# A block of cross-attention and a routed FFN on one core: FFN sums by ScalarE and accumulating DMAs, and another layout of a one-hot table

## The reference

```python
x = x + xattn(layernorm(x), ctx)          # 16 heads of 16, bias on q, k, v, o
xf = layernorm(x)                         # 4096 tokens of 256
shared = silu(xf @ sh_gate.T) * (xf @ sh_up.T) @ sh_down.T      # hidden 512
w, idx = top_k(softmax(xf @ gate_w.T), 2); w = w / sum(w)       # 8 experts
routed = sum over the two picks: w * (silu(xf @ eg[e].T) * (xf @ eu[e].T) @ ed[e].T)
out = x + shared + routed
```

## Time and profile before

| | us |
|---|---|
| median of 3 runs | 719.77 (718.18 to 723.15) |
| the profiled execution's own time | 715.89 |
| its span | 713.9 |
| PE busy | 614.5 (86%) |
| DVE busy | 440.9 (62%) |
| POOL busy | 394.1 (55%) |
| ACT busy | 346.4 (49%) |

### The profile page before, as it was taken

How to read it: one execution, slowest core, us unless ns; L and a number is a source line. 1 busy time by engine, 2 the same in 40 slices (tenths; PEclk the granted TensorE clock), 3 DMA queues, 4 the chain that set the end, 5 groups by cost and what they waited for, 6 DMA issues and landing times.

```text
span 713.9 us, 15571 instructions
## 1 busy us (share of the span) xinstructions
PE 614.5 (86%) x5294; PEld 416.7 (58%) x5294; DVE 440.9 (62%) x925; ACT 346.4 (49%) x561; POOL 394.1 (55%) x325
## 2 busy tenths in 40 slices
PE   4687668899978888977599899999999999999990
PEld 2243233566546554544356578877878787878780
DVE  5857886687787745779996644544454444454450
ACT  3797457787759763453224433333343333333330
POOL 5579687987864102121304446465756665666643
PEclk9899885598768998998989999999999999999996
DMA  8500000134212559434314766466656655656533
GB/s 262 176 2 1 0 1 1 32 70 107 42 39 46 141 150 248 142 100 115 96 59 131 159 91 105 69 106 92 106 85 99 103 99 92 108 93 107 91 46 37
DMA packets 103819, 65.08 MB, mean 91 GB/s; under 512 B 78594, under 2 KB 96964, under 8 KB 103748
## 3 DMA queue, kind: packets, MB, share of 16 engines
q1 hardware_dynamic: 88916, 40.86, 24.7%
q0 software_dynamic: 14832, 23.24, 19.3%
HBM read 29.47 MB, written 17.96 MB: 66 GB/s over the span
## 4 chain that ended last, share of the span: by engine, by line
PE 60%; DVE 20%; ACT 6%; issue 5%; DMA 3%; SPq 3%; POOL 2%; POOLq 0%; DVEq 0%; ACTq 0%
PE bank L1414 58%; DVE arena L966 3%; SPq L493 2%; DVE bank L1019 2%; DMA out<-w_stage,map_i 2%; DVE hidden L1299 2%; ACT arena L818 1%; PE bank L1764 1%; DVE arena L1276 1%; DVE arena L1272 1%; POOL arena L583 1%; ACT arena L733 1%; DVE x_sb L1355 1%; DVE bank L1305 1%; DVE arena L931 1%
## 5 line engine op out<-in xcount | busy, mean ns | idle before, releaser
L1414 PE MATMUL bank<-arena 128*128 128x34 f16 (+6 forms) x1284 | 138.1, 253 | 27.3 <-DVE bank L1019 11.4
L1414 PE MATMUL bank<-qx,arena 128*128 128x256 f16 (+1 forms) x1584 | 157.5, 288 | 3.2 <-ACT hidden L793 2.6
L674 POOL DMA_INDIRECT out<-w_stage,map_i x71 | 114.4, 1611 | 71.4 <-DMA out<-w_stage,map_i 32.6
L1414 PEld LDWEIGHTS bank<-qx,arena 128*128 (+1 forms) x1584 | 126.7, 101 | 25.4 <-issue 10.2
L1414 PEld LDWEIGHTS bank<-arena 128*128 128x128 f16 (+2 forms) x1284 | 74.3, 108 | 78.1 <-issue 47.3
L661 POOL DMA_INDIRECT qx<-rows_d,map_i x71 | 71.8, 1011 | 76.6 <-DVE lane_w L1375 33.7
L1383 DVE TENSOR_TENSOR hidden<-bank,hidden 128x512 f32<-128x512 f32 x71 | 49.1, 692 | 104.3 <-ACT hidden L900 104.3
L1414 PE MATMUL bank<-qx,w_sh 128*128 128x512 f16 x384 | 95.7, 399 | 19.8 <-DVE hidden L1299 17.7
L900 ACT ACTIVATE hidden<-bank 128x512 f32<-128x512 f32 x71 | 42.4, 597 | 129.4 <-PE bank L1414 129.4
L1414 PE MATMUL bank<-arena,w_stage 128*128 x852 | 104.6, 273 | 0.6 <-DVE w_stage L1402 0.4
L1414 PE MATMUL bank<-arena,qx 128*128 (+1 forms) x316 | 84.4, 390 | 14.3 <-DVE arena L966 12.6
(11 more groups left out here) (185 smaller groups left out, 725.1 us busy)
## 6 DMA issues: line engine op xcount, KB each, us to landing
w_stage<-in_w_all SPq DMA_DIRECT2D x27, 512.0 KB, 4.4
x_sb<-in_x SPq DMA_DIRECT2D x8, 512.0 KB, 8.1
rows_d<-arena SPq DMA_DIRECT2D x8, 512.0 KB, 4.0
out<-x_sb POOLq DMA_DIRECT2D x8, 512.0 KB, 5.6
qx<-rows_d,map_i POOLq DMA_INDIRECT x71, 3.1
qx<-qx SPq DMA_TRANSPOSE x71, 3.1
out<-w_stage,map_i POOLq DMA_INDIRECT x71, 3.9
arena<-arena SPq DMA_TRANSPOSE x32, 2.5
```

The lines of the kernel that those rows point to most:

```text
L674: pool.indirect_dma_start(out=out, out_offset=bass.IndirectOffsetOnAxis(ap=map_i[:, 1, i:i + 1], axis=0), in_=y_sb[:, r], in_offset=None, ...
L1414: return pe.matmul(o, a, b, start=first, stop=last, skip_group_check=not check)
```

## The change

**The sums.** `add_shared` is gone from VectorE. On ScalarE `take_shared(n)`, two copies of 128x512 from banks 4 and 5, puts the bare FFN sum of group n over the residual in `x_sb`, once `down_used` says the sum is ready and `x_stored[n]` says that the residual has been stored. It stands at the end of ScalarE's step (hc == 1), behind the cast of the high half. The residual is stored early: GpSimd issues `store_x(0..7)`, eight plain DMAs of 512 KB, right after attention. `store_out(n)` at its old places is now an accumulating DMA: it adds the sum to the rows in `out`.

**The table.** `hot_tile` has the order (2, 71, 8) in place of (16, 71): eight picks are innermost. `slot_iota` becomes (71, 8), made by a longer iota. `hot_lane` is unchanged. TensorE reads a pick's 71 columns with a step of 8 elements.

```diff
-        slot_iota = sb("slot_iota", [P, NS], F16)
+        slot_iota = sb("slot_iota", [P, NS, PI], F16)
...
-        hot_tile = carve([2, PC, NS], F16)
+        hot_tile = carve([2, PO, NS, PI], F16)
...
-            pool.iota(slot_iota[:, :], pattern=[[1, NS]], base=0, channel_multiplier=0,
+            pool.iota(slot_iota[:, :, :], pattern=[[1, NS], [0, PI]], base=0, channel_multiplier=0,
...
             def store_out(g):
                 pool.wait_ge(ffn_added, g + 1)
+                pool.dma_start(out_tiles[:, g * GT:(g + 1) * GT, :], x_sb[:, g * GT:(g + 1) * GT, :],
+                               accum_op=ALU.add).then_inc(out_stored, 16)
+
+            def store_x(g):
+                pool.wait_ge(y_added, GT // UT * (g + 1))
                 pool.dma_start(out_tiles[:, g * GT:(g + 1) * GT, :],
-                               x_sb[:, g * GT:(g + 1) * GT, :]).then_inc(out_stored, 16)
+                               x_sb[:, g * GT:(g + 1) * GT, :]).then_inc(x_stored[g], 16)
+
+            for g in range(NG):
+                store_x(g)
...
                 act.copy(h_h[:, k % 3], bank[2 + hc % 2][:, :]).then_inc(hh_ready, 1)
+                if hc == 1 and k > FC:
+                    take_shared(k // FC - 1)
+
+            def take_shared(n):
+                act.wait_ge(down_used, FC * (n + 1))
+                act.wait_ge(x_stored[n], 16)
+                for i in range(GT // 2):
+                    ins = act.copy(x_sb[:, GT * n + 2 * i:GT * n + 2 * i + 2, :],
+                                   bank[4 + i][:, :].rearrange("p (t c) -> p t c", t=2))
+                ins.then_inc(ffn_added, 1)
...
+            take_shared(NG - 1)
...
-                link3(dve.tensor_tensor(hot_tile[:, c % 2], slot_iota[:, :].unsqueeze(1).to_broadcast([P, PC, NS]),
-                                        pick_tile[:, at].unsqueeze(2).to_broadcast([P, PC, NS]), ALU.is_equal))
+                tiles, parts = [P, PO, NS, PI], "p (o i) -> p o i"
+                link3(dve.tensor_tensor(hot_tile[:, c % 2], slot_iota[:, :, :].unsqueeze(1).to_broadcast(tiles),
+                                        pick_tile[:, at].rearrange(parts, i=PI).unsqueeze(2).to_broadcast(tiles),
+                                        ALU.is_equal))
...
-                                  lane_val[:, :].unsqueeze(2).to_broadcast([P, PC, NS]),
+                                  lane_val[:, :].rearrange(parts, i=PI).unsqueeze(2).to_broadcast(tiles),
...
-                if hc == 1 and n > 0:
-                    add_shared(n - 1)
...
-            def add_shared(n):
-                dve.wait_ge(down_used, FC * (n + 1))
-                for i in range(GT // 2):
-                    xt = x_sb[:, GT * n + 2 * i:GT * n + 2 * i + 2, :]
-                    ins = dve.tensor_tensor(xt, xt, bank[4 + i][:, :].rearrange("p (t c) -> p t c", t=2), ALU.add)
-                ins.then_inc(ffn_added, 1)
...
-                    ins = mm(bank[6][:, c * NS:(c + 1) * NS], hot_lane[:, c % 2, j], hot_tile[:, c % 2, j],
+                    ins = mm(bank[6][:, c * NS:(c + 1) * NS], hot_lane[:, c % 2, j],
+                             hot_tile[:, c % 2, j // PI, :, j % PI],
```

More of the change, by code:

```diff
@@ L50, in build @@
     PC = 16
+    PI = 8
+    PO = PC // PI
     assert NT == 2 * PC and PC * P <= 2048
@@ L321, in build @@
         out_stored = sem("out_stored")
+        x_stored = [sem(f"x_stored{g}") for g in range(NG)]
         x2_stored = [sem(f"x2_stored{i}") for i in range(XB)]
@@ L1362, in _ @@
             hidden_low(FS - 1)
-            add_shared(NG - 1)
             def lane_weights(n):
```

## The result

The changed kernel takes 714.8 us at the median (711.0 to 723.1, 13 runs), the kernel before 720.8 on the same chip (715.5 to 723.2, 13 runs): a ratio of 0.9927 with an interval of 0.9899 to 0.9955, some 5.3 us less. The ratios leave out executions in a slower state of the chip, here one of the changed kernel's (723.1 us). The forecast was 11.3 us less. Repeated later, as a control beside other kernels, it gave 0.9966 [0.9928, 1.0004], some 2.5 us less, with an interval that just reaches no change. So it is faster, by 2.5 to 5.3 us, less than half of what was predicted.

A forecast was written before the change was run, and what follows sets the result against it. VectorE was taken to bound 298 to 372 us, almost only TensorE after 405 us. 3.6 + 3.6 + 0.8 + 1.6 + 4.7 - 1.0 - 1 - 1 = 11.3 us less gave a 708.5 us median, range 701 to 717.

The forecast's parts named there:

- 3.6 + 3.6 + 0.8 + 1.6: Shared steps: adds off VectorE 3.6, stalls in steps 13 and 17 3.6, step 20 0.8, low clock 1.6 us less.
- 4.7 for the tables: VectorE's table operations: eight at two elements per cycle instead of one, 4.7 us less (bounds 0 and 4.7).
- ScalarE's pair: Two PSUM copies per group on ScalarE, 1.2 us a pair, level with VectorE's old pair: taken as 0.
- Rival B: VectorE's shared steps: stalls move to other SBUF operations rather than go; 5.3 us less, 714.5 us, chance 0.13.
- So TensorE binds there in part: I give back 1.0 us (0 to 2.4): Steps 22 and 23: strided map matmuls make TensorE partly set the step, costing 1.0 us.
- 0 and a doubling of the chunk: TensorE's chunk of 16 strided map matmuls, 0.72 us before: bounds on its added time, at most +0.7 us.
- rival A: Tables gain nothing: operations stay at one element per cycle or strided matmuls take it back; 712.2 us, chance 0.16.
- I take -1: Transposes of x2 up to group 7, beside early and accumulating stores: net 1 us lost, bounds +3.5 and -10.
- 1.5 gained, half of 17 for the stores and 2 for the accumulating one: Transposes of x2: earlier low half gains 1.5 us; stores cost half of 17, the accumulating store at 274 costs 2.
- rival D: Group 7: transposes come earlier, TensorE's 3.55 us wait goes with its low clock; 17.8 us less, 702, chance 0.06.
- beside two stores that now accumulate: -1 (0 to -4): End of the shared stage: the last weight load, 5.21 us on the chain, loses 1 us to accumulating stores.
- rival C: DMA engines: stores delay transposes and weight loads; slower, 735 us at upper bounds, 724.5 middling; decides from 13.3 us, chance 0.07.

The follow-up runs named there:

- sums_only: The changed kernel with the table's old layout, keeping ScalarE sums, early stores and accumulating stores: 715.5 us, ratio 0.9955 to the kernel before.
- combo2: The changed kernel with early stores by SyncE inside attention, stores 4 and 5 ahead of the gathers, two picks innermost: 709.0 us, ratio 0.9817 to before.
- tables2: The kernel before with only the new tables, two picks innermost: 717.4 us, ratio 0.9942.
- no_early_plain: The changed kernel without early stores and with plain late stores, so the output lacks the residual: 705.8 us, ratio 0.9818 to the kernel before.
- after_again: The changed kernel, unaltered, run again as a control: 718.5 us, ratio 0.9966 to the kernel before.

## Why the prediction was wrong

**What held.** The forecast for steps 11 to 24 was 3.6 + 3.6 + 0.8 + 1.6 for the sums and 4.7 for the tables, 14.3; measured 9.8 by the sums alone and 14.6 with both. It holds step by step, and so is no luck: in sums_only step 13 is 2.9 us shorter and step 17 3.0 (forecast 1.2 + 1.8 each), step 20 1.0 (0.8), step 21 1.2 (1.2), and steps 14 and 18, where the clock's low stretches stood, 0.8 and 0.9 (1.0 and 0.6); the tables then take 1.2 us out of each of steps 20 to 23. The granted clock of 300 to 338 us is 1.00 instead of 0.87. ScalarE's pair cost nothing: from step 24 to 31, with two pairs in it, sums_only takes 27.6 us against 27.7. VectorE: DVE Perf Modes of the Trainium skill, "What auto-detection actually checks", asks for 16-bit tensors of step 1. The trace agrees, and shows besides that runs of two neighbours do. Rival B, the stalls moving, did not come about in steps 13, 17 and 20: sums_only alone has the 9.8.

**What failed** are three prices of what the change adds, put at 3.0 us in all and measured at 9.9. The ledger: 14.6 less and 2.7 + 3.7 + 3.4 more, 4.7 us less in the stage before rounding.
- "So TensorE binds there in part: I give back 1.0 us (0 to 2.4)". It is 3.7, outside even the bounds. The step that failed is the bound, "0 and a doubling of the chunk": the chunk tripled. Four chunks are 5.5 us longer together; the slack of TensorE hides 1.8. Of the 3.7 only 2.9 are the stride's (31.4 against the 28.5 of combo2 and tables2); 0.8 stay with chunks as short as before; there TensorE comes into VectorE's shorter steps late, and with a granted clock of 0.67 and 0.68 in step 22. This is half of rival A: the operations did double their rate and the strided matmuls took most of it back. The Trainium skill, SBUF — State Buffer, "Door 1: The DMA port swizzle", states a price for each access that crosses to a new 16-byte line. The direction agrees: a matmul of 71 columns takes 138 ns at 16 bytes from column to column, 77 at 8, 45 at 4 and at 2. But the same passage calls a step of 8 bf16 elements free and wants two hits per line for the full rate, and here 16 bytes cost three times as much and 8 bytes, two columns to a line, 1.7 times as much. The measurement decides.
- "I take -1" for the early stores (bounds +3.5 and -10). The result is -2.7. The -1 did not follow from its own terms: 1.5 gained, half of 17 for the stores and 2 for the accumulating one make -9. So it was a choice near the favourable end, and that it came within 1.7 is luck. The halves: the stores cost 7.7, near the 8.5 that the terms had and the -1 passed over; the earlier low half, with the clock behind it, is worth 5.0 rather than 1.5, as rival D had it. The trace reading that failed was of whom they hit: I looked at x2's transposes alone, and the first victims are attention's last two, 8.2 us instead of 2.5, with TensorE's projection behind them (4.3 us of the 7.7 lie in steps 0 to 2: 11.7 against no_early_plain's 7.4).
- "beside two stores that now accumulate: -1 (0 to -4)". It is 3.4, in other profiles of the same order 2.9 to 5.0. I took a value near the favourable end of a range, though by my own estimate two stores of at least 7.5 us each stood right ahead of the load. No profile gives the time to landing of an accumulating 512 KB store, so that estimate stays untested; its row was besides an indirect DMA, set against a plain one.

The mechanism of rival C was therefore at work, at 7.7 + 3.4 = 11.1 us below the 13.3 from which it decides. The own time of the profiled kernel before was also 5 us under the median of its runs on the result's chip (715.9 and 720.8); the forecast allowed for 3.9 of that.

**What stays open.** How large the cost of the early stores is, and how it is shared between bytes and order: the column 0 to 11 runs from 56.8 to 61.0 over six profiles whose programs do the same work there, the 51.7 stands in one profile, and a low clock behind a wait adds to small differences. Why after_again spent 4.5 us more behind the first slot than the first profile. Whether accumulation or the two-fold traffic in `out` slows the load was not told apart.

## What to carry to other kernels

When work is moved off a bound engine, price what the new form adds with the same care as what it removes, each at the place where it lands: here the removed part was forecast within 0.3 us and the added part at a third of its size. When the terms of a working add up to -9, do not write down -1 without a reason. Move only what is on the path: three of the eight sums held all of the gain in VectorE's steps, and a layout needs only the two neighbours that were enough for the fast rate here. Issue bulk stores where nothing urgent shares the DMA engines, not where a chain of transposes or the last load of a stage runs.

## What the runs showed of the hardware

- A moving operand read with a step: at a granted clock of 1.00, 16 matmuls of 71 f16 columns take 0.72 us at 2 bytes from column to column, 0.73 at 4, 1.23 at 8 and 2.21 at 16. The kernel before has one chunk of 1.17 at 2 bytes, in step 22 with a granted clock of 0.50.
- A two-input f16 operation of 1,136 elements takes 0.74 us when its innermost run has 2, 4 or 8 neighbours, and 1.33 to 1.34 when one input has step 0 innermost. Beside a GpSimd tensor_tensor it was up to 3.26 us long.
- Seven plain stores of 512 KB issued in a row bring a DMA transpose from 2.5 to 8.2 us and a store of the other queue from 4.0 to 14.4. An accumulating store of 512 KB keeps GpSimd 1.27 to 1.54 us at issue, a plain one 0.75 to 1.00.
- TensorE's granted clock behind a wait: in step 10 it is 0.67 in the kernel before (3.55 us idle before the gate) and the step takes 10.4 us; in no_early_plain, with 1.50 us idle, it stays at 1.00 and the step takes 6.0.
- The eleven profiles whose programs do the same work up to about 220 us start the shared stage anywhere between 233.1 and 241.7 us. The granted clock differs there: from 90 to 120 us it is 0.72 in the kernel before and 0.67 in sums_only, whose stage starts 8.4 us later. A single pair of spans can hide, or invent, several microseconds. Stage lengths are steadier, but not exact: programs with the same work differ by up to 4.2 us up to step 11, and the changed kernel's two profiles by 4.5 us behind the first slot.
